# Low halves of the first expert's chunks on GpSimd, and idle products within the find

## The chip, the cores and the metric

The kernel runs on one core of one Trainium2 chip. The metric is the device time of one execution in microseconds, lower is better; for the kernel before it is the median of three executions. A profile of one more execution gives the span, from the first to the last instruction, and what each engine did in it.

## The reference

```python
x = x + xattn(layernorm(x), ctx, ctx)        # x, ctx: (4, 512, 512), 8 heads
x = x + ffn(layernorm(x), Wg, bg, W1, W2)

def ffn(x, Wg, bg, W1, W2):                  # 2048 tokens, 4 experts, H = 2048
    logits = flat_x @ Wg + bg
    top_vals, top_idx = top_k(logits, 2)     # two experts a token
    probs = softmax(those two, -inf elsewhere)
    for i in range(4):
        score = where(expert i is among the two, probs[:, i], -inf)
        sel_p, sel_idx = top_k(score, 512)   # capacity: the 512 best tokens
        tok = flat_x[sel_idx]
        y = (gelu(tok @ W1[i]) @ W2[i]) * sel_p
        out = out.at[sel_idx].add(y)
```

Everything is float32.

## The kernel before, in words

Each engine has one instruction list in program order, and semaphores join the lists. There are four stages.

**Attention** works on 16 units of 128 rows. The last units also give `x2n`, the normalised rows (stored to `x2n_dram`, line 416), and the router's logits. Toward its end ScalarE makes the high halves of the first two weight chunks (`split_hi(0, c)`, lines 707 and 744).

**Keys and search.** From the logits VectorE makes a key for each token and expert (`keys_of`, line 953, first for 12 units, then for the last 4), copies the last keys wide (line 1056, semaphore `key_done`), and TensorE transposes them into PSUM. Six rounds then search four thresholds: in each VectorE counts half of the keys against `thr` (L1071) beside ScalarE, which counts the other half (L760), TensorE adds the counts up, and VectorE makes the next `thr` (semaphore `thr_done`, once ahead of the first round and once behind each of the first five).

**The find.** VectorE turns the thresholds into slots and makes one-hot matrices in four quarters (`one_hot`, L1164). TensorE multiplies them with a payload of token numbers and probabilities (`find`, line 1451, 16 products, four behind each quarter). VectorE reads off the row indices (`slots_of`, line 1179). GpSimd fetches the 512 token rows of expert 0 in four indirect DMAs of 128 rows (`gather_x`, line 606, L610), and then as many rows of the output (L621). TensorE transposes each block of rows when it is there (L1466, with two idle products between blocks), ScalarE copies it as `xt_hi` (L773), VectorE makes `xt_lo` (L1227).

**Experts.** A float32 product is made of three: high times high, high times low, low times high. `up` (line 1469) makes 12 products for 128 hidden channels, `down` (line 1495) 12 more. They take the weights in chunks of 256 hidden channels: `load_chunk` (SyncE) brings 1 MB into one of two `raw` buffers in two DMAs (L396, L398), ScalarE rounds it into `w_hi` (L711), and the difference, `w_lo`, is made by VectorE as one 128x2048 instruction (`split_lo`, L1208). For chunk 0 of expert 0 GpSimd makes the difference in four 128x512 pieces (`first_low`, line 556, L560), one behind each of the thresholds 2 to 5. VectorE makes that of chunk 1 behind `slots_of` (line 1224). Each finished chunk adds one to `wlo_done`. SyncE waits for it ahead of each further chunk's load (line 478), and TensorE ahead of the products that use the chunk (line 1472). VectorE, too, waits for two of them ahead of `credit` (line 1234).

**Idle products** (line 1342) multiply a zero tile of 128x128 with one of 128x512 into a bank that nobody reads: 9 ahead of the find, 14 behind it.

GpSimd's list around the change is: the last residual, two `finish`, the four pieces, waits for the stored rows, `gather_x(0)`.

Of the kernel before, what the change touches and what calls it, by code (L numbers as in the profile page):

```python
# [27 lines left out]
UNITS = N_TOK // P  # L28
# [76 lines left out]
def xattn_moe_kernel(nc, x, ctx_in, Wg, bg, W1, W2, consts, out):  # L105
# [6 lines left out]
    with ExitStack() as stack:  # L112
        def sem(name):
            return stack.enter_context(nc.semaphore(name))
# [124 lines left out]
        four = stack.enter_context(nc.psum_tensor("four", [P, 4, 512], F32))  # L239
# [58 lines left out]
        x2n_done = sem("x2n_done")  # L298
# [11 lines left out]
        key_done = sem("key_done")  # L310
        key_t = sem("key_t")
        thr_done = sem("thr_done")
# [17 lines left out]
        wlo_done = sem("wlo_done")  # L330
# [157 lines left out]
        def _(pool):  # L488
# [49 lines left out]
            def finish(u):  # L538
                n = number(u)
                pool.wait_ge(var2_done, n + 1)  # L540
                inv_sqrt(rstd2[u[1]][:, :], var2_e[u[1]][:, :], 1).then_inc(rstd2_done, 1)
# [14 lines left out]
            def first_low(c, q):  # L556

                pool.wait_ge(whi_done, c + 1)
                part = slice(q * HALF // 2, (q + 1) * HALF // 2)
                low_part = nc.gpsimd.tensor_tensor(w_lo[c][:, part], raw[c][:, part], w_hi[c][:, part].bitcast(F32),  # L560
                                                   ALU.subtract)
                if q == 3:
                    low_part.then_inc(wlo_done, 1)
# [30 lines left out]
            residual((UNITS // 2 - 1, 0))  # L594
            finish((UNITS // 2 - 1, 0))
            finish((UNITS // 2 - 1, 1))
            for q in range(4):
                pool.wait_ge(thr_done, q + 2)
                first_low(0, q)
            pool.wait_ge(logit_done, UNITS)  # L600
            pool.wait_ge(x2_stored, 16 * UNITS)
            for n in range(2):
# [193 lines left out]
        def _(dve):  # L796
# [407 lines left out]
            def split_lo(e, c):  # L1204

                n = CHUNKS * e + c
                dve.wait_ge(whi_done, n + 1)
                nc.vector.tensor_tensor(w_lo[c % SPLIT_BUFS][:, :], raw[c % RAW_BUFS][:, :],  # L1208
                                        w_hi[c % SPLIT_BUFS][:, :].bitcast(F32), ALU.subtract
                                        ).then_inc(wlo_done, 1)  # L1210
# [9 lines left out]
                dve.wait_ge(xthi_done, g + 1)  # L1220
                nc.vector.tensor_tensor(lo, bank, hi.bitcast(F32), ALU.subtract).then_inc(xt_split, 1)

            dve.wait_ge(wlo_done, 1)
            split_lo(0, 1)
            for t in range(ST):
                dve.wait_ge(xthi_done, t + 1)
                nc.vector.tensor_tensor(xt_lo[:, 0, :, t * P:(t + 1) * P],  # L1227
# [39 lines left out]
        def _(pe):  # L1267
# [74 lines left out]
            def idle_products(n):  # L1342

                for _ in range(n):
                    nc.tensor.matmul(four[:, 3, :], idle_in[:, 0:P], idle_in[:, :], start=True, stop=True)  # L1345
# [102 lines left out]
                             ).then_inc(pre_ready, 1)  # L1448
            idle_products(9)

            def find(e, bank):

                pe.wait_ge(pay_done, e + 1)
                for t in range(UNITS):
                    if t % (UNITS // QUARTERS) == 0:
                        pe.wait_ge(oh_done, QUARTERS * e + t // (UNITS // QUARTERS) + 1)
                    last = nc.tensor.matmul(bank[:, 0:ST * PAY], onehot[:, t, :],
                                            pay[:, bass.ds(e, 1), t, :, :].rearrange("p a s c -> p (a s c)"),
                                            start=(t == 0), stop=(t == UNITS - 1))
                last.then_inc(found_ready, 1)  # L1460
# [50 lines left out]
                        last.then_inc(acc_ready, 1)  # L1511


            find(0, four[:, 0, :])
            idle_products(14)
            for t in range(ST):
                pe.wait_ge(x_gathered[t], 16)
                transpose_tokens(t, (bank_t, bank_m, *two)[t])
# [7 lines left out]
            def expert(e, last):  # L1526
                for m in range(MT):
                    if m < MT - 1:
                        up(e, m + 1, e % 2)
                    elif not last:  # L1530
                        pe.wait_ge(xt_split, ST * (e + 2))
                        up(e + 1, 0, (e + 1) % 2)
                    down(e, m)
                    if not last and m == FIND_AT:
                        pe.wait_ge(xt_split, ST * (e + 1))
                        find(e + 1, bank_m)
                    if not last and XT_AT <= m < XT_AT + ST:
                        pe.wait_ge(x_gathered[m - XT_AT], 16 * (e + 2))
                        pe.wait_ge(xt_split, ST * (e + 1) + m - XT_AT - 1)
                        transpose_tokens(m - XT_AT, (bank_t, bank_m)[m % 2])  # L1540
# [22 lines left out]
```

## Time and profile before

| | |
|---|---|
| runs | 615.79, 617.82, 618.09 us; median 617.82 |
| profiled execution | 617.56 us, span 615.8 us |
| TensorE busy | 580.6 us, 94% of the span |
| VectorE busy | 353.3 us, 57% |
| ScalarE busy | 281.2 us, 46% |
| GpSimd busy | 187.4 us, 30% |
| mean granted TensorE clock | 0.973 |
| the last keys copied wide | 210.88 us |
| rounds' first and last count (L1071) | 213.75 and 223.20 us |
| first fetch of token rows | 233.70 us |
| first expert product | 247.18 us |

Times within the execution are counted from the start of the span. PE is TensorE's products and PEld its weight loads, DVE is VectorE, ACT ScalarE, POOL GpSimd, SP SyncE. A row of the timeline gives start and length, both in us, the engine, the line of the kernel, the operation, what it writes and reads, and in brackets how long the engine had been idle and what it waited for. A row with a count (x4) stands for so many instructions from the first one's start to the last one's end. A granted clock of 1.00 is 2.4 GHz and 0.50 is 1.2 GHz.

### The profile page before, as it was taken

The numbers are of one execution on the slowest core, as the hardware profiler recorded it, in microseconds if no ns is written. First come the engines' busy times: TensorE is split into PE (matmuls) and PEld (weight loads), VectorE is DVE, ScalarE is ACT, GpSimd is POOL, SyncE is SP. The second block draws the span as 40 slices with busy tenths as digits, with TensorE's granted clock in tenths as the row PEclk, the third lists the DMA queues.
The fourth block names the chain that finished last, engine by engine and source line by source line (L and its number), as shares of the span: only waits on it lengthen the run. The fifth ranks groups of instructions, "written<-read, shape, count | busy, mean of one in ns | idle before, by whom it ended". The sixth has DMA issues, their size and how long they took to land.

```text
span 615.8 us, 8885 instructions
## 1 busy us (share of the span) xinstructions
PE 580.6 (94%) x2924; PEld 410.6 (67%) x2924; DVE 353.3 (57%) x698; ACT 281.2 (46%) x421; POOL 187.4 (30%) x142
## 2 busy tenths in 40 slices
PE   8999999999998735999999999999999999999994
PEld 4445555555554413788888888888888888888883
DVE  6889998998988683543444633444534255423212
ACT  3877777767776231533333334325324324333220
POOL 8465566466552226000300420400510401500002
PEclk9999999999999857999999999999999999999998
DMA  4523323323213125223323352333452522541001
GB/s 152 206 70 124 117 97 118 128 87 120 87 54 104 68 69 193 81 86 121 119 86 136 137 195 78 122 113 106 158 182 68 163 110 84 176 152 68 1 0 68
DMA packets 46600, 67.80 MB, mean 110 GB/s; under 512 B 8560, under 2 KB 25072, under 8 KB 46576
## 3 DMA queue, kind: packets, MB, share of 16 engines
q1 hardware_dynamic: 42736, 54.91, 26.5%
q0 software_dynamic: 3840, 12.59, 6.0%
q8 instruction: 13, 0.21, 0.1%
q14 instruction: 11, 0.09, 0.1%
HBM read 54.77 MB, written 12.64 MB: 109 GB/s over the span
## 4 chain that ended last, share of the span: by engine, by line
PE 69%; DVE 5%; DMA 1%; issue 1%; ACT 1%; POOL 0%; POOLq 0%; DVEq 0%
PE two L1478 29%; PE four L1508 9%; PE four L1507 9%; PE four L1505 9%; PE two L1310 3%; PE four L1300 2%; PE two L1322 1%; DMA x_got<-x2n_dram,idx_all 1%; DVE junk L1071 1%; PE four L1345 1%; PE bank_t L1338 1%; PE bank_t L1466 1%; PE bank_m L1466 1%; PE bank_t L1330 0%; PE four L1411 0%
## 5 line engine op out<-in xcount | busy, mean ns | idle before, releaser
L784 ACT ACTIVATE h_f<-two 128x512 f32<-128x512 f32 x64 | 38.3, 598 | 228.0 <-PE two L1478 228.0
L1240 DVE TENSOR_TENSOR h_lo<-h_f,h_hi 128x512 fp32r<-128x512 f32 x64 | 44.1, 690 | 122.8 <-ACT h_hi L785 122.8
L1478 PE MATMUL two<-xt_hi,w_hi 128*128 (+1 forms) x256 | 101.7, 397 | 0.7 <-ACT xt_hi L773 0.7
L1508 PE MATMUL four<-w_hi,h_lo 128*128 128x512 f32 x256 | 100.3, 392 | 0.0
L1507 PE MATMUL four<-w_lo,h_hi 128*128 128x512 f32 x256 | 100.3, 392 | 0.0
L1505 PE MATMUL four<-w_hi,h_hi 128*128 128x512 f32 x256 | 100.3, 392 | 0.0
L1478 PE MATMUL two<-xt_hi,w_lo 128*128 (+1 forms) x256 | 100.0, 391 | 0.0
L1478 PE MATMUL two<-xt_lo,w_hi 128*128 (+1 forms) x256 | 99.9, 392 | 0.0
L678 ACT ACTIVATE prob<-four,rnorm 128x512 f32<-128x512 f32 x128 | 77.6, 690 | 28.0 <-POOL rnorm L490 19.1
L1208 DVE TENSOR_TENSOR w_lo<-raw,w_hi 128x2048 fp32r<-128x2048 f32 x31 | 71.0, 2290 | 23.4 <-ACT w_hi L711 23.4
L490 POOL TENSOR_TENSOR rnorm<-ss_max,power 128x8 f32<-128x8 f32 x32 | 64.5, 2017 | 48.8 <-DVE ss_max L833 43.8
L631 POOL DMA_INDIRECT out<-o_got,idx_all x16 | 20.1, 1257 | 163.8 <-DVE o_got L1261 161.3
L610 POOL DMA_INDIRECT x_got<-x2n_dram,idx_all x16 | 25.0, 1560 | 139.1 <-DVE idx_all L1195 123.8
L1310 PE MATMUL two<-prob,v_t 128*64 128x512 f32 x256 | 61.9, 604 | 0.0
L711 ACT ACTIVATE w_hi<-raw 128x2048 fp32r<-128x2048 f32 x32 | 61.3, 1918 | 0.0
L1478 PEld LDWEIGHTS two<-xt_hi,w_hi 128*128 128x128 f32 x256 | 48.1, 188 | 11.1 <-ACT xt_hi L773 0.9
L1508 PEld LDWEIGHTS four<-w_hi,h_lo 128*128 128x128 f32 x256 | 48.0, 188 | 10.8
L1505 PEld LDWEIGHTS four<-w_hi,h_hi 128*128 128x128 f32 x256 | 48.0, 188 | 10.8
L1478 PEld LDWEIGHTS two<-xt_hi,w_lo 128*128 128x128 f32 x256 | 48.1, 188 | 10.7
L1507 PEld LDWEIGHTS four<-w_lo,h_hi 128*128 128x128 f32 x256 | 48.0, 188 | 10.7
L1478 PEld LDWEIGHTS two<-xt_lo,w_hi 128*128 128x128 f32 x256 | 48.2, 188 | 9.8
L881 DVE TENSOR_TENSOR half_sum<-prob 128x512 f32<-128x512 f32 x64 | 41.5, 690 | 0.1
(183 smaller groups left out, 761.5 us busy)
## 6 DMA issues: line engine op xcount, KB each, us to landing
raw<-in_L_ffn_W SPq DMA_DIRECT2D x64, 512.0 KB, 4.2
x_all<-in_x SPq DMA_DIRECT2D x16, 256.0 KB, 2.7
c_sb<-in_ctx SPq DMA_DIRECT2D x16, 256.0 KB, 2.7
out<-x_all SPq DMA_DIRECT2D x16, 256.0 KB, 2.1
x2n_dram<-x2n SPq DMA_DIRECT2D x16, 256.0 KB, 2.0
p_inv<-inv_dram SPq DMA_DIRECT2D x30, 128.0 KB, 2.8
few<-p_sum SPq DMA_DIRECT2D x30, 2.0 KB, 2.1
cst<-in_consts SPq DMA_DIRECT2D x1, 423.5 KB, 5.2
```

The costliest lines, as they stand in the source:

```text
L490: return nc.gpsimd.tensor_tensor(dst, src, power[:, 0:n], ALU.pow)
L678: last = nc.scalar.activation(prob[h][t][:, :], s_ps[:, 2 * (t % 2) + h, :], ACT.Exp, scale=rnorm[u[1]][:, 0, t, h:h + 1])
L711: nc.scalar.activation(w_hi[c % SPLIT_BUFS][:, :], raw[c % RAW_BUFS][:, :], ACT.Copy).then_inc(whi_done, 1)
L784: nc.scalar.activation(h_f[m % 2][:, :], z_ps[m % 2][:, :], ACT.Gelu)
L881: nc.vector.tensor_tensor(half_sum[h][n][:, :], prob[h][2 * n][:, :], prob[h][2 * n + 1][:, :], ALU.add).then_inc(halves_done[h], 1)
L1208: nc.vector.tensor_tensor(w_lo[c % SPLIT_BUFS][:, :], raw[c % RAW_BUFS][:, :], w_hi[c % SPLIT_BUFS][:, :].bitcast(F32), ALU.subtract).then ...
L1240: nc.vector.tensor_tensor(h_lo[m % 2][:, :], h_f[m % 2][:, :], h_hi[m % 2][:, :].bitcast(F32), ALU.subtract).then_inc(h_split, 1)
L1310: last = nc.tensor.matmul(o_ps[0][DH * h:DH * (h + 1), :], v_t[u[1]][:, t, h, :], prob[h][t][:, :], start=(t == 0), stop=(t == TT - 1))
L1478: return nc.tensor.matmul(z[:, :], w_part[c][:, w], x_k, start=start, stop=stop)
L1505: nc.tensor.matmul(acc_ps[:, t, :], h_hi[m % 2][:, h], w_hi[c][:, w], start=(m == 0), stop=False)
L1507: nc.tensor.matmul(acc_ps[:, t, :], h_hi[m % 2][:, h], w_lo[c][:, w], start=False, stop=False)
L1508: last = nc.tensor.matmul(acc_ps[:, t, :], h_lo[m % 2][:, h], w_hi[c][:, w], start=False, stop=(m == MT - 1))
```

## The change

All eight pieces of chunks 0 and 1 go to GpSimd: two once all rows of `x2n` are made, one once the last keys are copied, five behind the thresholds 2 to 6. `first_low(0, q)` is chunk 0 and `first_low(1, q)` chunk 1. VectorE's `split_lo(0, 1)` and the wait ahead of it go. In the first find two idle products stand ahead of each of the last three quarters' waits, and 20 instead of 14 stand behind it. The finds of the other experts have none.

```diff
@@ GpSimd @@
             finish((UNITS // 2 - 1, 0))
             finish((UNITS // 2 - 1, 1))
-            for q in range(4):
-                pool.wait_ge(thr_done, q + 2)
+            pool.wait_ge(x2n_done, UNITS)
+            for q in range(2):
                 first_low(0, q)
+            pool.wait_ge(key_done, 2)
+            first_low(0, 2)
+            for q in range(3, 8):
+                pool.wait_ge(thr_done, q - 1)
+                first_low(q // 4, q % 4)
             pool.wait_ge(logit_done, UNITS)
@@ VectorE @@
-            dve.wait_ge(wlo_done, 1)
-            split_lo(0, 1)
             for t in range(ST):
                 dve.wait_ge(xthi_done, t + 1)
@@ TensorE @@
-            def find(e, bank):
+            def find(e, bank, idle=0):
                 pe.wait_ge(pay_done, e + 1)
                 for t in range(UNITS):
                     if t % (UNITS // QUARTERS) == 0:
+                        if t:
+                            idle_products(idle)
                         pe.wait_ge(oh_done, QUARTERS * e + t // (UNITS // QUARTERS) + 1)
...
-            find(0, four[:, 0, :])
-            idle_products(14)
+            find(0, four[:, 0, :], 2)
+            idle_products(20)
```

## Rows read from the trace of the kernel before

**Rows 1.** TensorE's groups from 247.1 us on: busy us, mean ns, idle before.
```profile
L1478 PE MATMUL two<-xt_hi,w_hi 128*128 (+1 forms) x256 | 101.7, 397 | 0.7 <-ACT xt_hi L773 0.7
```

**Rows 2.** The chain that ended last, 229 to 250 us: start, us, what.
```profile
233.70 7.83 DMA x_got<-x2n_dram,idx_all
...
246.05 0.45 PE two L1466 x4
...
246.53 0.61 ACT xt_hi L773
...
247.18 3.02 PE two L1478 x12
```

**Rows 3.** The timeline, 213 to 236 us: start, us, engine, line, operation.
```profile
213.70 1.26 POOL L560 TENSOR_TENSOR w_lo<-raw,w_hi 128x512 fp32r<-128x512 f32 x1 [8.58 <-DVE thr L1112]
213.75 1.28 DVE L1071 TENSOR_SCALAR_CACHE_REDUCE junk<-four,thr 128x1024 bf16<-128x1024 f32 x1
...
223.20 1.28 DVE L1071 TENSOR_SCALAR_CACHE_REDUCE junk<-four,thr 128x1024 bf16<-128x1024 f32 x1
...
232.64 2.28 DVE L1208 TENSOR_TENSOR w_lo<-raw,w_hi 128x2048 fp32r<-128x2048 f32 x1
233.70 2.32 POOL L610 DMA_INDIRECT x_got<-x2n_dram,idx_all  x1 [11.60 <-issue]
235.08 0.37 SPq L396 DMA_DIRECT2D raw<-in_L_ffn_W  x1
```

**Rows 4.** Windows: busy of PE, PEld, DVE, ACT, POOL, clock, DMA share, GB/s.
```profile
236.00:239.00 3.00, 0.00 (x0) 0.00 (x0) 0.00 (x0) 0.00 (x0) 2.08 (x4) 0.86 0.94 315
...
303.30:304.70 1.40, 1.40 (x7) 1.12 (x6) 0.52 (x1) 1.40 (x3) 1.09 (x2) 1.00 0.66 187
304.70:306.30 1.60, 1.60 (x8) 1.29 (x7) 0.49 (x2) 1.25 (x1) 1.30 (x2) 1.00 0.63 164
```

**Rows 5.** The timeline of expert 1's fetches: GpSimd, then VectorE.
```profile
301.70 1.00 POOL L610 DMA_INDIRECT x_got<-x2n_dram,idx_all  x1 [56.53 <-DVE idx_all L1195]
303.00 1.00 POOL L610 DMA_INDIRECT x_got<-x2n_dram,idx_all  x1 [0.30 <-issue]
...
306.05 3.10 POOL L610 DMA_INDIRECT x_got<-x2n_dram,idx_all  x1 [0.30 <-issue]
...
305.98 2.29 DVE L1208 TENSOR_TENSOR w_lo<-raw,w_hi 128x2048 fp32r<-128x2048 f32 x1 [1.11 <-ACT w_hi L711]
```

**Rows 6.** The timeline, 205 to 213 us, on VectorE.
```profile
205.15 0.55 DVE L918 TENSOR_SCALAR x2n<-x_all,mv,rstd 128x512 f32<-128x512 f32 x1 [0.67 <-POOL rstd L490]
...
208.81 0.16 DVE L1051 SCALAR_TENSOR_TENSOR rest<-count,excess 128x1 f32<-128x1 f32 x1 [1.41 <-ACT junk_a L760]
...
210.88 0.43 DVE L1056 COPY key_w<-key 128x512 f32<-128x512 f32 x1
...
212.86 0.16 DVE L1083 SCALAR_TENSOR_TENSOR enough<-count,rest 128x1 bf16<-128x1 f32 x1
```

**Rows 7.** The timeline, 226 to 235 us: idle products and the find.
```profile
226.50 4.05 PE L1345 MATMUL four<-idle_in 128*128 128x512 bf16 x9
...
231.38 0.26 PE L1457 MATMUL four<-pay,onehot 128*128 128x20 bf16 x4 [0.32 <-DVE onehot L1164]
...
232.09 3.18 PE L1345 MATMUL four<-idle_in 128*128 128x512 bf16 x14
```

**Rows 8.** Windows again, for TensorE's busy time and granted clock.
```profile
204.00:207.40 3.40, 3.36 (x24) 2.24 (x22) 1.83 (x8) 0.98 (x2) 0.55 (x1) 0.99 0.62 231
...
227.90:231.30 3.40, 3.03 (x15) 1.13 (x13) 3.26 (x10) 0.00 (x0) 0.00 (x0) 0.50 0.00 0
...
234.70:238.10 3.40, 0.58 (x3) 0.08 (x1) 0.22 (x1) 0.00 (x0) 2.79 (x3) 1.00 0.58 183
238.10:241.50 3.40, 0.00 (x0) 0.00 (x0) 0.00 (x0) 0.00 (x0) 2.55 (x3) 0.51 0.99 363
241.50:244.90 3.40, 3.33 (x12) 2.40 (x13) 0.69 (x1) 1.07 (x2) 2.73 (x3) 0.50 0.76 240
```

## The prediction

> **What bounds the kernel now.** I read the page first, then the groups of instructions behind the routing stage, then the chain of waits through that stage, then the timelines along the chain.
>
> The page shows TensorE busy for most of the span, but that average hides two kinds of stretch. From 247.18 us to the end the expert loop never lets TensorE wait: the six matmul groups have 0.7 us of idle time ahead of them together, all ahead of the first product [rows 1]. So whatever moves the first expert product moves the end one for one, and nothing inside the loop can give or take anything as long as the chunks' halves are made in time. Ahead of it, from the keys to the first product, TensorE waits for others.
>
> The chain there: GpSimd begins the first fetch of token rows at 233.70, and 7.83 us later the rows are there for TensorE; then four blocks are transposed with idle products between, ScalarE takes the last one (0.61 us), and the first expert product starts at 247.18 [rows 2]. The long piece is the fetch, and the timeline shows what lies beside it. VectorE starts its 128x2048 subtraction (the low half of chunk 1) at 232.64 for 2.28 us; the first fetch instruction, begun inside it, takes 2.32 us. When the subtraction ends, at 234.92, SyncE issues the load of chunk 3, two DMAs, the first at 235.08 [rows 3]. The fetch instruction ends at 236.02, so its rows queue behind 1 MB: from 236 to 239 the DMA engines are 94% busy at 315 GB/s [rows 4]. Its rows come 5.5 us after the instruction has ended.
>
> The same fetch in expert 1 shows what it costs undisturbed [rows 4, 5]. Its instruction takes 1.00 us, the next starts 1.30 us after it, and only the fourth, with VectorE's 2.29 us subtraction beside it, takes 3.10 us. The first one's instruction ends at 302.70 and its 262 KB (187 GB/s times 1.4 us) have moved by 304.7, 2.0 us later; the second ends at 304.00, and its rows have moved by 306.3, 2.3 us later.
>
> **The change, part by part.**
>
> *VectorE's subtraction of chunk 1 goes.* It removes one instruction of 2.28 us [rows 3]. VectorE itself was waiting for tokens afterwards, so its own time is worth nothing. What it held up is: the first fetch instruction falls from 2.32 to 1.00 us [rows 3, 5], 1.3 us. Bounds: 0, if that length belongs to the first fetch of a program, and 1.3; I take 1.3, since the fourth fetch of expert 1 stretches beside the same subtraction.
>
> *The load of chunk 3 moves.* GpSimd's eighth piece starts with the last threshold at about 223.2, where VectorE's last count stands [rows 3], and takes 1.26 us: chunk 3 is issued near 224.6 and, by the 315 GB/s above, is in by some 228.5. Chunk 2 goes out after the fourth piece, near 215.0, where no other load is under way. Both are over long before the fetch, and neither queues behind anything else on SyncE. Landing after the instruction's end: 2.0 to 2.3 us instead of 5.5. Lower end 2.0; upper end 5.5 if the first fetch is slow by itself; I take 2.3, expert 1's value inside a series.
>
> *Four more pieces on GpSimd*, 1.26 us each [rows 3]. Two follow the last normalised unit (205.15 + 0.55 = 205.70) and are done near 208.5; one follows the keys' copy (210.88 + 0.43 = 211.31) [rows 6]; one the last threshold. The new waits hold nothing but further pieces and the fetch on GpSimd's queue. The last of them is met near 223.2 and the fetch waits until 232.6 for its indices, so pieces and waits cost GpSimd nothing. Those who wait for the pieces (SyncE's two loads, the first expert product) get them earlier than before. For VectorE: the count beside a piece takes 1.28 us, and without one also 1.28 us [rows 3], so a piece beside a count costs nothing. The nearest instruction with two SBUF inputs behind the first two is at 208.81, and behind the third, which starts about 211.5 and ends about 212.8, at 212.86 [rows 6]. I take 0; bounds 0 and the 1.26 us of one piece. The Trainium skill (SBUF — State Buffer, "SBUF: two separate sides") has it that a GpSimd operation and a VectorE operation with two SBUF inputs exclude each other for a whole instruction, the later one being blocked. By that rule the sum is the same only while the pieces keep these places; if one slips it costs its full length. No row of before has such a pair in the search; the stretched fetches agree with it.
>
> *Six idle products within the first find.* One takes 0.45 us at 1.2 GHz (9 in 4.05) and 0.227 us at 2.4 GHz (14 in 3.18) [rows 7]. The clock is at the lower level until 231.3 [rows 8], so the first two cost 0.9 or a little less and the other four 0.9: 1.7 together. The pauses for the one-hot quarters, some 0.3 us each [rows 7], hide some 0.9. The find ends 0.8 us later, and it is on the chain. Bounds: 0.45 (all at the upper level) and 1.8 (all at the lower).
>
> *20 idle products instead of 14.* The find ends at 233.0, so they last until 237.6. The first rows are there at 234.5 + 1.0 + 2.0 = 237.5. That is a cost of 0.1 that is not on the chain, since the last rows decide.
>
> **The sum.** First fetch at 233.70 + 0.8 = 234.5. Fourth at + 3 x 1.30 = 238.4, its instruction ends at 239.4, its rows are there at 241.7. A block takes 0.45 us to transpose at the upper level and two idle products 0.45, less than the 1.30 us between fetches, so TensorE waits for the fetches. From the fourth block's transpose to the first expert product it was 247.18 - 246.05 = 1.13 us [rows 2]: 242.8. The gain is 4.35 us. The profiled execution took 617.56 us (span 615.8), so 613.2; it lies 0.26 us under the median, so I forecast a median of 613.4. What is late next is the fourth fetch, paced by GpSimd's instructions; before it was the DMA engines' backlog.
>
> **The rivals.**
>
> *The clock falls in the token stage.* In 234.7 to 238.1 TensorE was busy for 0.58 us, and in the next stretch the granted clock was 0.51; in 204 to 207.4 it was busy nearly throughout and kept it [rows 8]. After the change the 4.1 us from 237.6 to 241.7 hold three blocks and six products, some 2.7 us: between these two. If it falls near 241.5 and stays low until 244.9, as it did before [rows 8], the last block loses some 0.4 us and the products from 242.8 on lose half of 2.1 us: 1.4 less, a gain of 2.95, 614.9.
>
> *The find runs wholly at the lower level.* The clock was low until 231.3 [rows 8]. If it rises some 2.5 us later, all six products run at the lower level, and the find loses 1.8 us instead of 0.8: a gain of 3.35, 614.5.
>
> *The first fetch is slow by itself.* Then the load of chunk 3 hid behind a latency and only 1.3 - 0.8 = 0.5 us is gained: 617.3. Against it: expert 1's 2.0 us, and 94% busy engines.
>
> *The change doesn't bring chunk 3 forward*, because the second count of low halves comes late: the eighth piece would have to slip by 8 us. It would leave 0.5 us: 617.3.
>
> *The pieces hold up VectorE's chain (slower).* Place: from the keys to the last threshold every VectorE instruction waits for the one before it. Price: 1.26 us for each piece that gets ahead of a two-input instruction. From the fourth held piece on the gain of 4.35 is gone (5.0); all eight held, 10.1 us, give 623.6. Against it: the four pieces of before cost none of the counts anything [rows 3]. The Trainium skill's rule of SBUF's two sides is what would do it.
>
> **How the numbers follow.** Forecast as summed 0.55; clock falls in the token stage 0.22; find at the lower level 0.08; fetch slow by itself 0.10; load not brought forward 0.02; pieces hold VectorE 0.03. A measurement of this kernel can tell about 0.5% (3.1 us) from no change. The forecast lies 1.3 us beyond that, the clock's fall on its edge, the find at the lower level just beyond. So: faster 0.66 (0.51 of the forecast, 0.09 of the clock, 0.06 of the find), slower 0.03, same 0.31. Range: the bounds of find and landing allow 5.0 us of gain, and the runs before reach 2.0 us under their median, of which I allow 1.0: 611.8. At the top the clock's case with 1.3 us more for a piece that holds VectorE: 616.2. That leaves out 0.15.
>
> **What would show it.** Right: the first fetch instruction takes about 1.0 us and its start moves by +0.8; no VectorE 128x2048 subtraction before the loop; the chunk loads issued near 215.0 and 224.6, and DMA traffic from 236 on of the fetches alone; the last transposes near 241.7; the first expert product near 242.8, and the loop as long as before. Wrong: first rows more than 3 us after their instruction; a granted clock of 0.5 between 241 and 245; counts of over 1.28 us or an idle VectorE in front of the two-input instructions in the search; the find over 1.8 us longer.

## The result, and the profile after

The changed kernel takes 614.67 us (median of 5 executions, 613.27 to 614.77), the kernel before beside it 617.35 us (5 executions, 615.79 to 618.09). The ratio is 0.9944, with a 95% interval of 0.9918 to 0.9969: 2.7 us, some 0.6%. The forecast was 613.4 us, the range 611.8 to 616.2. The profiled execution took 613.68 us, its span is 611.9 us against 615.8.

The page: TensorE's busy time, with 12 instructions more and a higher share of a shorter span.

```profile
PE 582.0 (95%) x2936; PEld 410.6 (67%) x2936; DVE 350.9 (57%) x697; ACT 280.9 (46%) x421; POOL 190.9 (31%) x146
```

TensorE's first group from 243.2 us on. It answers to [rows 1]: again 0.7 us ahead of the first product and nothing behind it.

```profile
L1483 PE MATMUL two<-xt_hi,w_hi 128*128 (+1 forms) x256 | 101.8, 398 | 0.7 <-issue 0.7
```

The timeline behind the last threshold, to the first expert product. It answers to [rows 2, 3].

```profile
223.36 1.28 DVE L1076 TENSOR_SCALAR_CACHE_REDUCE junk<-four,thr 128x1024 bf16<-128x1024 f32 x1
223.39 1.26 POOL L560 TENSOR_TENSOR w_lo<-raw,w_hi 128x512 fp32r<-128x512 f32 x1 [1.13 <-DVE thr L1127]
...
224.82 0.37 SPq L396 DMA_DIRECT2D raw<-in_L_ffn_W  x1
...
232.46 4.48 PE L1348 MATMUL four<-idle_in 128*128 128x512 bf16 x20
232.65 0.17 DVE L1188 TENSOR_REDUCE row<-four 128x4 f32<-128x8 f32 x1 [0.56 <-PE four L1462]
...
234.07 1.24 POOL L615 DMA_INDIRECT x_got<-x2n_dram,idx_all  x1 [9.42 <-issue]
235.62 1.01 POOL L615 DMA_INDIRECT x_got<-x2n_dram,idx_all  x1 [0.30 <-issue]
...
237.70 0.42 PEld L1471 LDWEIGHTS bank_t<-cst,x_got 128*128 128x128 f32 x4 [1.25 <-DMA x_got<-x2n_dram,idx_all]
...
238.24 1.00 POOL L615 DMA_INDIRECT x_got<-x2n_dram,idx_all  x1 [0.30 <-issue]
...
241.91 0.42 PEld L1471 LDWEIGHTS two<-cst,x_got 128*128 128x128 f32 x4 [0.63 <-DMA x_got<-x2n_dram,idx_all]
...
243.25 0.19 PEld L1483 LDWEIGHTS two<-xt_hi,w_hi 128*128 128x128 f32 x1 [0.93 <-issue]
```

The eighth piece runs beside the last count, which still takes 1.28 us, and the load of chunk 3 goes out at 224.82, where it was 235.08. The first fetch instruction takes 1.24 us instead of 2.32. Its rows are there for TensorE at 237.70, 2.4 us after its end; the fourth block's at 241.91. The first expert product starts at 243.25 instead of 247.18.

The find, with two idle products ahead of each later quarter (against [rows 7]):

```profile
230.65 0.81 PE L1348 MATMUL four<-idle_in 128*128 128x512 bf16 x2
...
231.30 0.25 PE L1462 MATMUL four<-pay,onehot 128*128 128x20 bf16 x4
...
231.40 0.59 PE L1348 MATMUL four<-idle_in 128*128 128x512 bf16 x2
...
231.83 0.25 PE L1462 MATMUL four<-pay,onehot 128*128 128x20 bf16 x4
```

Windows over the token stage (busy of PE, PEld, DVE, ACT, POOL, then granted clock, DMA share, GB/s), against [rows 4, 8]:

```profile
238.10:241.50 3.40, 2.59 (x17) 1.35 (x15) 1.38 (x2) 1.32 (x3) 2.65 (x3) 1.00 0.71 200
241.50:244.90 3.40, 2.57 (x13) 1.80 (x12) 2.29 (x6) 2.35 (x3) 2.33 (x3) 1.00 0.73 210
236.00:239.00 3.00, 2.03 (x11) 0.79 (x9) 0.00 (x0) 0.60 (x1) 2.39 (x3) 1.00 0.70 188
```

The clock keeps the upper level where it was 0.50 before, and from 236 to 239 the DMA engines move 188 GB/s of fetched rows instead of 315 GB/s of chunk and rows.

**A yardstick.** Executions of one kernel differ by 3 us and more, which is more than the parts of this change. The profiles show where. In all twelve of this study the span from the first expert product to the end is 368.5 to 368.7 us. The start of the last keys' copy (L1056, L1061 in the changed kernel) lies anywhere from 209.93 to 212.38 us, and at 212.59 in e8, where a third piece ahead of it costs 1.07 us. In the other kernels at most the first two pieces stand ahead of it, and they cost nothing there: from the last normalised unit to the copy it is 5.73 us before (205.15 to 210.88) and 5.75 after (205.30 to 211.05). Between the two lies what the change touches. So for each kernel I give, besides the ratio, the stretch from the keys' copy to the first expert product, out of its one profile.

| kernel | keys' copy | indices read | first fetch | first block | expert product | stretch | ratio (95%) |
|---|---|---|---|---|---|---|---|
| before | 210.88 | 232.28 | 233.70 | 241.57 | 247.18 | 36.30 | 1 |
| changed | 211.05 | 232.65 | 234.07 | 237.70 | 243.25 | 32.20 | 0.9944 (0.9918 to 0.9969) |
| e1 | 210.59 | 231.96 | 233.39 | 237.05 | 242.65 | 32.06 | 0.9944 (0.9930 to 0.9959) |
| e2 | 211.45 | 232.85 | 234.28 | 237.94 | 243.74 | 32.29 | 0.9935 (0.9921 to 0.9950) |
| e3 | 210.64 | 232.03 | 233.45 | 237.64 | 246.72 | 36.08 | 1.0018 (1.0004 to 1.0032) |
| e4 | 210.72 | 232.11 | 233.53 | 238.25 | 244.39 | 33.67 | 0.9956 (0.9943 to 0.9969) |
| e5 | 212.02 | 233.39 | 234.81 | 242.29 | 248.84 | 36.82 | 1.0017 (0.9999 to 1.0035) |
| e6 | 211.15 | 232.52 | 233.95 | 237.49 | 243.17 | 32.02 | 0.9952 (0.9934 to 0.9971) |
| e7 | 212.38 | 233.76 | 235.18 | 238.89 | 244.35 | 31.97 | 0.9951 (0.9933 to 0.9969) |
| e8 | 212.59 | 234.09 | 235.52 | 239.08 | 244.83 | 32.24 | 0.9960 (0.9944 to 0.9975) |
| e9 | 209.93 | 231.32 | 232.75 | 237.39 | 244.16 | 34.23 | 0.9958 (0.9944 to 0.9972) |
| e10 | 211.41 | 232.81 | 234.23 | 237.87 | 243.73 | 32.32 | 0.9942 (0.9919 to 0.9965) |

"Indices read" is the start of VectorE's L1183 (L1188), "first block" the start of the first transpose of token rows. The change is worth 36.30 - 32.20 = 4.10 us on this yardstick. It rests on one profile of the kernel before; only the changed kernel has two (32.20 and 32.06 us).

The executions give less. The kernel before has 55 on record, of mean 616.80 us, and the changed kernel 11, of mean 613.80: 3.0 us, with a 95% interval of about 2.4 to 3.6. So the stretch of the kernel before was probably shorter than 36.30 us in many of its executions. Which size is right between 3 and 4 us stays open; that the change gains does not.

### The profile page after: what moved, and what is told of

It is laid out like the page before. It is cut to its first block, busy times and chain, and to the rows that moved or that the text cites. A ratio compares the mean times of both kernels' runs of the same rounds, so it can differ in the third digit from the quotient of the medians.

```text
span 611.9 us, 8914 instructions
## 1 busy us (share of the span) xinstructions
PE 582.0 (95%) x2936; PEld 410.6 (67%) x2936; DVE 350.9 (57%) x697; ACT 280.9 (46%) x421; POOL 190.9 (31%) x146
## 4 chain that ended last, share of the span: by engine, by line
PE 70%; DVE 4%; issue 2%; ACT 1%; DMA 1%; POOL 0%; POOLq 0%; DVEq 0%
PE two L1483 29%; PE four L1512 10%; PE four L1513 10%; PE four L1510 9%; PE two L1313 3%; PE four L1303 2%; PE two L1325 1%; PE four L1348 1%; DVE junk L1076 1%; PE bank_t L1341 1%; DMA x_got<-x2n_dram,idx_all 1%; PE four L1414 1%; PE bank_t L1333 0%; PE bank_t L1471 0%; PE bank_m L1471 0%
## 5 line engine op out<-in xcount | busy, mean ns | idle before, releaser
L1213 DVE TENSOR_TENSOR w_lo<-raw,w_hi 128x2048 fp32r<-128x2048 f32 x30 | 68.7, 2290 | 23.3 <-ACT w_hi L716 23.3
```

## The experiments

**e1: the changed kernel once more.** No edit.

> The changed kernel once more, for a second profile beside it. In the first, the first expert product starts at 243.25 us (247.18 before) and the span is 611.9; three of its five executions had a span of 612.9. Theory A (fetch): the chain up to the first expert product is shorter by about 4 us in every execution, and the 1 us between executions is TensorE's clock changing at another moment. Expected: ratio 0.993 to 0.997, first expert product at 243.2 to 244.4, and if the span is above 612.5, a stretch with a granted clock of 0.5 that the first profile does not have, or the same stretch at another time. Theory B (clock): the idle products bring the gain and the fetch little; this run can't tell, e2 can.

613.34 us against 616.82, 0.9944 (0.9930 to 0.9959). The stretch is 32.06 us, within 0.14 of the first profile; of the 0.7 us by which its span is shorter, 0.46 are older than the keys' copy and 0.14 are this, and the end differs by 0.1. The first expert product came at 242.65 us, 0.55 ahead of the range expected. The expectation about a clock that moves was only half right: the low stretch that the first profile has ahead of the keys (200.6 to 204) is missing here, but no low stretch lies in the token stage of either.

**e2: without the idle products.**

```diff
-            find(0, four[:, 0, :], 2)
-            idle_products(20)
+            find(0, four[:, 0, :])
+            idle_products(14)
```

> The changed kernel without its new idle products: none within the find, 14 behind it. Theory A: the find ends 0.3 to 0.4 us earlier, the fetch instructions and the landing are as in the changed kernel, rows of the fourth block visible near 241.5. TensorE idles from 235.3 to 237.4, so the clock may fall near 238 or 241.5; if it does, the first expert product comes 1 to 2 us later than in the changed kernel (ratio to before 0.995 to 0.999); if it does not, 0.3 us earlier (ratio 0.993). Theory B: most of the gain is gone, ratio 0.999 or more, with landings as late as before.

613.02 us, 0.9935 (0.9921 to 0.9950): all of the gain is there, and theory B falls. The timeline and a window (same columns as above):

```profile
234.28 1.24 POOL L615 DMA_INDIRECT x_got<-x2n_dram,idx_all  x1 [9.20 <-issue]
...
237.94 0.42 PEld L1471 LDWEIGHTS bank_t<-cst,x_got 128*128 128x128 f32 x4 [2.58 <-DMA x_got<-x2n_dram,idx_all]
...
240.13 0.63 PE L1348 MATMUL four<-idle_in 128*128 128x512 bf16 x1
...
243.74 0.19 PEld L1483 LDWEIGHTS two<-xt_hi,w_hi 128*128 128x128 f32 x1 [0.92 <-ACT xt_hi L778]
```

```profile
238.90:242.30 3.40, 3.10 (x12) 2.12 (x12) 1.38 (x2) 1.15 (x3) 2.53 (x3) 0.52 0.72 196
```

TensorE idles ahead of the first block, and the clock falls behind it, as the prediction feared for the changed kernel. The expectation priced that at 1 to 2 us, and it costs little: the fetches still set the pace of the first three blocks, and the clock is back at the fourth. The indices are read 0.20 us earlier after the keys' copy than in the changed kernel (21.40 against 21.60), and the product comes 0.09 later. So the idle products' gain and cost cancel within 0.1 us.

**e3: the load of chunk 3 late again.** ScalarE, idle there, makes a copy of 128x2048 that nothing uses, and SyncE waits for it (through a new semaphore, `late`) ahead of that load.

```diff
@@ ScalarE, behind the last count @@
+            act.wait_ge(idx_done, 1)
+            nc.scalar.activation(w_lo[2][:, :], w_hi[0][:, :].bitcast(F32), ACT.Copy).then_inc(late, 1)
@@ SyncE @@
                     sp.wait_ge(wlo_done, e * CHUNKS + c + 1)
+                    if c == 1:
+                        sp.wait_ge(late, 1)
```

> The changed kernel, with the load of chunk 3 held back until ScalarE has made a copy of 128x2048 (1.92 us) behind the first indices, so that it is issued at about 235.1 as before, with nothing on VectorE beside the fetch. Theory A (backlog): the first fetch instruction stays at 1.0 to 1.3 us, but its rows come at 239 to 241 instead of 237.7; TensorE idles, the clock falls, the first expert product comes 1.5 to 3 us later than in the changed kernel (ratio to before 0.996 to 0.999). Theory C (the subtraction's hold on the fetch instruction is the whole gain): no more than 0.3 us later, ratio 0.993 to 0.995.

617.70 us, 1.0018 (1.0004 to 1.0032): nothing of the gain is left, with all of the low halves on GpSimd and all idle products in place. Timeline, then windows:

```profile
233.45 1.24 POOL L618 DMA_INDIRECT x_got<-x2n_dram,idx_all  x1 [9.20 <-issue]
234.56 0.37 SPq L397 DMA_DIRECT2D raw<-in_L_ffn_W  x1
...
237.64 0.66 PE L1476 MATMUL bank_t<-cst,x_got 128*128 128x128 f32 x4 [1.54 <-DMA x_got<-x2n_dram,idx_all]
...
241.50 1.12 PE L1476 MATMUL bank_m<-cst,x_got 128*128 128x128 f32 x4 [2.77 <-DMA x_got<-x2n_dram,idx_all]
...
246.72 0.19 PEld L1488 LDWEIGHTS two<-xt_hi,w_hi 128*128 128x128 f32 x1 [1.09 <-ACT xt_hi L783]
```

```profile
236.00:239.00 3.00, 1.20 (x7) 0.58 (x6) 0.04 (x1) 0.60 (x1) 2.08 (x4) 1.00 0.93 332
240.00:246.00 6.00, 4.50 (x16) 3.07 (x16) 1.38 (x2) 1.19 (x2) 3.00 (x3) 0.50 0.84 276
```

The first block is hardly later than in the changed kernel (4.19 us after the fetch began, 3.63 there). The second is: it comes at 241.50, 3.86 us behind the first, where it was 1.50. The load was out at 234.56, between the starts of the first and the second fetch instruction, and its 1 MB stands ahead of the second block, at 332 GB/s. TensorE waits 2.77 us, the clock falls, and the three blocks left are then transposed with their idle products at 1.2 GHz, 1.7 us a block, although their rows may be there. Theory C falls; the expected shape was off by one block, and the loss was larger than the 1.5 to 3 us.

**e4: a subtraction beside the fetch, the load early.**

```diff
+            nc.vector.tensor_tensor(w_lo[2][:, :], w_hi[0][:, :].bitcast(F32), w_hi[1][:, :].bitcast(F32),
+                                    ALU.subtract)
             for t in range(ST):
                 dve.wait_ge(xthi_done, t + 1)
```

> The changed kernel with one more 128x2048 subtraction on VectorE where split_lo(0, 1) stood (its result is not used); the load of chunk 3 stays early. Theory A: the first fetch instruction takes 2.2 to 2.4 us, all four rows come 1.0 to 1.2 us later, the first expert product 1.0 to 1.2 us later (more by 1 if the clock falls). Theory C: about 3.5 us later, all of the gain gone.

614.57 us, 0.9956 (0.9943 to 0.9969):

```profile
232.47 2.28 DVE L1228 TENSOR_TENSOR w_lo<-w_hi 128x2048 fp32r<-128x2048 f32 x1
233.53 2.32 POOL L615 DMA_INDIRECT x_got<-x2n_dram,idx_all  x1 [9.21 <-issue]
...
238.25 0.42 PEld L1473 LDWEIGHTS bank_t<-cst,x_got 128*128 128x128 f32 x4 [2.34 <-DMA x_got<-x2n_dram,idx_all]
...
244.39 0.19 PEld L1485 LDWEIGHTS two<-xt_hi,w_hi 128*128 128x128 f32 x1 [0.93 <-issue]
```

The fetch instruction takes 2.32 us again, 1.08 more, and the first block comes 1.09 us later behind it (4.72 against 3.63). The stretch is 1.47 us longer than the changed kernel's, as the clock fell at 239.6 here. This is the price of the subtraction alone, with the change's 20 idle products behind the find.

**e5: the idle products alone, on the kernel before.** The change's edits to `find`, and at its call:

```diff
-            find(0, four[:, 0, :])
-            idle_products(14)
+            find(0, four[:, 0, :], 2)
+            idle_products(20)
```

> The kernel before with the idle products of the change alone (two ahead of each later quarter of the first find, 20 behind it). Theory A (the load ahead of the fetch is what costs): the rows still land 5 us or more behind their fetch instruction, the find ends 0.3 to 0.8 us later, ratio to before 0.999 to 1.002. Theory B (the clock's upkeep brings the gain): the clock stays at the upper level over the transposes, ratio 0.995 or less.

617.65 us, 1.0017 (0.9999 to 1.0035):

```profile
233.75 2.28 DVE L1208 TENSOR_TENSOR w_lo<-raw,w_hi 128x2048 fp32r<-128x2048 f32 x1
234.81 2.32 POOL L610 DMA_INDIRECT x_got<-x2n_dram,idx_all  x1 [11.58 <-issue]
...
242.29 0.71 PEld L1468 LDWEIGHTS bank_t<-cst,x_got 128*128 128x128 f32 x4 [5.10 <-DMA x_got<-x2n_dram,idx_all]
...
248.84 0.19 PEld L1480 LDWEIGHTS two<-xt_hi,w_hi 128*128 128x128 f32 x1 [0.93 <-ACT xt_hi L773]
```

The first block comes 5.2 us after its instruction's end, and the first expert product comes 36.82 us behind the keys' copy. Theory B would have needed 0.995. The stretch is 0.52 us longer than before, though the find is not later (21.37 us after the copy) and the first block lands 0.4 us sooner behind it. The clock makes the rest: it is low from 240.8 to 247.6, into the fourth block, where before it was back at 245.0, at the start of the third. From the first block to the expert product it takes 6.55 us instead of 5.61. So the stretch of a kernel with the late landing moves with the moment at which the clock comes back.

**e6: 20 products behind the find, none within.**

```diff
-            find(0, four[:, 0, :], 2)
+            find(0, four[:, 0, :])
```

> The changed kernel with no idle products within the find, but 20 behind it. Theory A: within the uncertainty of the changed kernel, at best 0.3 us faster (the find ends 0.3 to 0.4 us earlier, and so does everything behind it); ratio to before 0.993 to 0.995. Theory B: 1 us or more slower than the changed kernel, as the clock rises later.

613.75 us, 0.9952 (0.9934 to 0.9971), stretch 32.02: 0.18 us less than the changed kernel, from the find. By time it can't be told from the changed kernel.

**e7: idle products in the search too.** e6, and four products behind each small product of the first five rounds, into `two[1]`.

```diff
                     nc.tensor.matmul(bank_m[:, 0:1], block_b[:, :], enough[:, :], start=True, stop=True
                                      ).then_inc(n_ready, 1)
+                    for _ in range(4):
+                        nc.tensor.matmul(two[1][:, :], idle_in[:, 0:P], idle_in[:, :], start=True, stop=True)
```

> The changed kernel with no idle products within the find, 20 behind it, and four behind each small product of the first five search rounds, into a bank that is free there. It asks what the clock is worth in search and find. Theory A: the clock stays at the upper level from the keys to the experts; the search itself is VectorE's and stays as long (within 0.2 us), the first quarter's products start as soon as the quarter is there, the transposes run at the upper level in every execution: 0.3 to 1.0 us faster than the changed kernel, ratio to before 0.992 to 0.994. Against it: if a round's small product has to wait for idle products, 0.2 us or more a round are lost.

613.99 us, 0.9951 (0.9933 to 0.9969), stretch 31.97. The expectation was wrong: the clock did not stay up through the search, and no 0.3 to 1.0 us were gained. The four products of a round show the clock:

```profile
214.68 1.02 PE L1447 MATMUL two<-idle_in 128*128 128x512 bf16 x4
...
221.47 1.87 PE L1447 MATMUL two<-idle_in 128*128 128x512 bf16 x4
```

The upper level is gone at 221.2 all the same, and comes back only at 231.3; in the other kernels it went between 212.5 and 216.9. In e6 it lasted 2.9 us behind the keys' copy, here 8.8, the first three of the five groups of four. The rounds are as long as without them (11.14 us from the first count to the last, 11.13 in e6), since a round is VectorE's and ScalarE's. The find, here at the upper level, is not shorter either (21.38 us after the copy, 21.37 in e6). So a higher clock in these rounds and in the find is worth nothing that shows.

**e8: the third piece beside the last keys.**

```diff
-            pool.wait_ge(key_done, 2)
+            pool.wait_ge(logit_done, UNITS)
             first_low(0, 2)
```

> The changed kernel with the third piece moved forward: it waits for the last logits instead of the copied keys, so it runs beside VectorE's last key instructions, most of which read two tiles of SBUF. If a GpSimd piece and such an instruction exclude each other (the lock rule of the prediction's slower rival), the chain of key instructions is 0.5 to 1.3 us longer and shows a gap or a stretched instruction beside the piece, and the time is as much longer than the changed kernel's. If they share the port at no cost, the key instructions keep their starts relative to the last logits within 0.1 us and the time is the changed kernel's.

614.41 us, 0.9960 (0.9944 to 0.9975). VectorE and GpSimd in this kernel, then VectorE's same instructions in the changed one:

```profile
209.71 0.22 DVE L966 TENSOR_TENSOR cmp_o<-logits,cst 128x64 f32<-128x64 f32 x1
209.76 1.31 POOL L560 TENSOR_TENSOR w_lo<-raw,w_hi 128x512 fp32r<-128x512 f32 x1 [0.98 <-DVE logits L845]
209.85 1.29 DVE L968 TENSOR_TENSOR cmp_b<-logits 128x64 f32<-128x64 f32 x1
211.06 0.21 DVE L970 TENSOR_TENSOR cmp_a<-logits 128x64 f32<-128x64 f32 x1
```

```profile
209.38 0.22 DVE L968 TENSOR_TENSOR cmp_b<-logits 128x64 f32<-128x64 f32 x1
209.52 0.22 DVE L970 TENSOR_TENSOR cmp_a<-logits 128x64 f32<-128x64 f32 x1
```

A comparison of 0.22 us takes 1.29 us: it begins 0.09 us after the piece and ends with it, and both its inputs are in SBUF. So the two exclude each other for the piece's full length, as the Trainium skill says (SBUF — State Buffer, "SBUF: two separate sides"); here the trace agrees, with 1.07 us lost on the keys' chain. That loss lies ahead of the keys' copy, so the stretch (32.24) does not show it.

**e9: the kernel before, the load held back.** The subtraction stays beside the first fetch.

```diff
                     sp.wait_ge(wlo_done, e * CHUNKS + c + 1)
+                    if c == 1:
+                        sp.wait_ge(x_gathered[ST - 1], 16)
```

> The kernel before with one wait more: SyncE holds the load of chunk 3 until the fourth block of token rows is there. VectorE's subtraction stays beside the first fetch. Theory A (backlog): the rows of the first block come 2.0 to 2.7 us after their instruction has ended instead of 5.5, the fourth block near 242.5; TensorE idles from 235.3 to about 238.5, so the clock may fall. First expert product at 243.5 to 246, ratio to before 0.994 to 0.998, about what e4_dummy_sub gave. The loop stays as long as before, since chunk 3 is first needed 8 us later than it can be there. If the load is not what delays the rows: ratio 0.999 to 1.001.

614.19 us, 0.9958 (0.9944 to 0.9972):

```profile
232.75 2.32 POOL L612 DMA_INDIRECT x_got<-x2n_dram,idx_all  x1 [11.60 <-issue]
...
237.39 0.71 PEld L1468 LDWEIGHTS bank_t<-cst,x_got 128*128 128x128 f32 x4 [3.56 <-DMA x_got<-x2n_dram,idx_all]
...
242.04 0.37 SPq L396 DMA_DIRECT2D raw<-in_L_ffn_W  x1
...
244.16 0.19 PEld L1480 LDWEIGHTS two<-xt_hi,w_hi 128*128 128x128 f32 x1 [0.94 <-issue]
```

With the load behind the fetches the first block comes 2.3 us after its instruction's end, although the instruction still takes 2.32 us. The stretch is 34.23, 2.07 us less than before. That is with 14 idle products, and a clock low from 236.4 to 243.2, over all four blocks; what the change gains beyond it is the subtraction and this clock. e10, below, differs from e9 in that the subtraction leaves the fetch too, and its stretch is 1.91 us shorter.

**e10: the kernel before, VectorE's subtraction behind the token blocks.**

```diff
-            dve.wait_ge(wlo_done, 1)
-            split_lo(0, 1)
             for t in range(ST):
                 dve.wait_ge(xthi_done, t + 1)
...
                                         ).then_inc(xt_split, 1)
+            dve.wait_ge(wlo_done, 1)
+            split_lo(0, 1)
             for e in range(1, E):
```

> The kernel before with VectorE's subtraction for chunk 1 moved behind its four token blocks; no piece of it goes to GpSimd and no idle product is added. The load of chunk 3, which waits for it, moves to about 247. Theory A (what counts is only that neither the subtraction nor the load stands beside the first fetch): the first fetch instruction takes 1.0 to 1.3 us, the rows are there as in the changed kernel, first expert product 3 to 4 us earlier than before, less 0.3 to 0.6 us that VectorE then is late with the first h_lo: ratio 0.993 to 0.996. If GpSimd's share matters by itself, it falls short of that: 0.997 or more.

613.78 us, 0.9942 (0.9919 to 0.9965), stretch 32.32:

```profile
234.23 1.24 POOL L610 DMA_INDIRECT x_got<-x2n_dram,idx_all  x1 [11.60 <-issue]
...
243.73 0.19 PEld L1478 LDWEIGHTS two<-xt_hi,w_hi 128*128 128x128 f32 x1 [0.92 <-ACT xt_hi L773]
...
244.32 2.28 DVE L1208 TENSOR_TENSOR w_lo<-raw,w_hi 128x2048 fp32r<-128x2048 f32 x1
...
246.76 0.37 SPq L396 DMA_DIRECT2D raw<-in_L_ffn_W  x1
```

Two lines moved give what the whole change gives. The subtraction runs under the first expert products, the load goes out at 246.76, and TensorE waits for neither: the rest of the span is 368.7 us. The clock is low from 238.8 to 242.0, much as in e2, and the stretch is as long as there. GpSimd's four more pieces are one way of getting the two things away from the fetch, and show no other effect. Taken in this order the parts add up: 2.07 us for the load (e9), 1.91 for the subtraction (e10), 0.12 for the rest of the change.

No version beats the changed kernel by more than can be measured; e2, e6, e7 and e10 are its equals.

## Why the prediction was right

**What bounds, and one for one.** Right. The rest behind the first expert product was 368.6 us before and after.

**The subtraction.** Forecast: the first instruction from 2.32 to 1.00 us. It took 1.24, as in every kernel with nothing beside it; 0.24 of the 1.3 us belong to the program's first fetch. e4 gives 1.08 us for it, and 1.47 with what the clock then does.

**The load of chunk 3.** Right, and the larger part: e3 has the load alone and loses all of the gain, e9 takes the load alone away and gains 2.07 us. The two parts don't add up (1.47 and 3.88 us against 4.10), since the load alone is enough: with it in place, taking the subtraction away gains 0.22 us (before 36.30, e3 36.08), and the clock falls over the last three blocks, a cost that the prediction did not price. The prediction took the load for a matter of the first block's landing, 2.3 us instead of 5.5. The fourth block took 2.7 us behind its instruction's end (239.24 to 241.91), 0.4 more than the row of expert 1 gave.

**The pieces.** Right at 0 for the places they have: the last key instructions and the counts are as long as before, and behind the third piece (211.56 to 212.82) the two-input instruction starts at 213.02, 1.97 us after the keys' copy, as it did at 1.98. e8 shows the rule behind the slower rival at work, at 1.07 us for one piece. The rival's price was right, its places were not met.

**The find.** The term was too large: +0.8 us forecast, and the indices are read 0.20 us later after the keys' copy (21.60 against 21.40). The step that failed is the pauses: I took a group of four find products for 0.26 us of TensorE, its length in the timeline, where the idle products follow 0.10 us after its start. One-hot quarters come every 0.60 us (231.38 and 231.98 before). A group and its two idle products take 0.53 us at the upper level (231.30 to 231.83 in the changed kernel) and fit; at the lower level they take 0.80 (230.50 to 231.30) and overrun by 0.20, which is the whole cost. In e1, where the clock rose earlier, it is nil (21.37). So even the lower bound of 0.45 was too high.

**The blocks.** From the last block's transpose to the expert product it took 1.34 us (241.91 to 243.25), not 1.13. Most of that is a misreading of the kernel before. The prediction took 246.05, the row of the chain that ended last; the timeline has the same transposes start at 245.89, so it was 1.29 us there too. The other 0.05 come with a last block that TensorE waited for. The row of the kernel before, then that of the changed one:

```profile
245.89 0.60 PE L1466 MATMUL two<-cst,x_got 128*128 128x128 f32 x4
```

```profile
241.91 0.66 PE L1471 MATMUL two<-cst,x_got 128*128 128x128 f32 x4
```

**The sum.** The find cost 0.6 less than forecast, the first instruction 0.24 more, the landing 0.4, the last block 0.2: 4.35 + 0.6 - 0.24 - 0.4 - 0.2 = 4.1, which is what the yardstick shows; between the two profiles' first products it is 3.93. That the misses nearly cancel is luck. The medians differ by 2.7 us in the first comparison and 3.5 in e1, and all executions together by 3.0: the forecast of 4.4 us against the median was too large by 0.9 to 1.7 us, and 613.4 lies 1.3 us under the measured median. (Its own last step, 613.2 and 0.26, gives 613.5.) Each of the two intervals still holds 4.1 us (0.9934), all executions together do not. What the gap between the profiles and the executions is made of is open; e5 shows one thing that moves the stretch of such a kernel by 0.9 us, the clock's return.

**The rivals.** The clock did not fall in the token stage: TensorE was busy for 2.59 of 3.4 us from 238.1 on and kept 1.00. In e2 and e10 it did, and cost 0.27 and 0.30 us (32.29 and 32.32 against e6's 32.02), not 1.4, as the fetches' pace hides most of it. The find ran at the lower level until its second quarter, for the 0.20 us above and not 1.8. The fetch is not slow by itself, but for 0.24 us.

## What to carry to other kernels

The indirect fetch that this stage waits for needed two things out of its way: a VectorE subtraction with two SBUF inputs while GpSimd runs the fetch's instructions, and a 1 MB load issued between them. Here taking away the subtraction alone gained next to nothing (0.22 us), taking away the load alone 2.07, and the load left with the subtraction that released its buffer. Where moving the offender behind the fetch (e10) costs nothing downstream, that is as good as moving it to another engine ahead of it. When executions differ by more than the change, measure between two marks of the trace, one ahead of the change and one behind it after which the rest is rigid. Then profile both kernels more than once, and compare with the mean of many executions: here the marks gave 4.1 us and the executions 3.0.

## What the runs showed of the hardware that I had not expected

A 1 MB load issued 1.1 us after the first of four indirect fetches began left the first block's landing nearly alone (4.19 against 3.63 us) and delayed the second by 2.4 us more (e3). Four idle products in each search round kept TensorE's clock at the upper level for 8.8 us behind the keys' copy (2.9 in e6), but not through the search: it fell at 221.2 us with the same pattern of work still going on, and was back only at 231.3, near the end of the nine products ahead of the find (e7). The first indirect fetch of the program takes 1.24 us, the three behind it 1.00 to 1.02.
